# Half of an attention product in rounded parts, the bias as a matrix product, and the experts' data in six loads

## The reference, cut to what matters

```
q, k, v = 1x1 convolutions of x (4 images, 256 channels, 32 x 32 pixels)
energy  = q . k                       # every pixel against every pixel of its image
attn    = softmax(energy, last axis)  # over 32 columns, for each of the 32 rows of keys
x       = gamma * (attn x v) + x
t       = tokens of x                 # 4096 tokens of 256
u       = layer_norm(t)
t       = t + u @ W1 + (memory @ u) @ W2 + bias     # memory: band of 32, within one image
t       = t + mixture of 32 experts, 2 chosen per token, of layer_norm(t)
```

## Time and profile before

| | us |
|---|---|
| median of 3 runs (438.37 to 448.01) | 442.87 |
| the profiled execution's own time | 442.4 |
| its span, first to last instruction | 440.7 |
| PE busy | 371.4 (84%) |
| DVE busy | 331.7 (75%) |
| POOL busy | 286.8 (65%) |
| ACT busy | 272.5 (62%) |

### The profile page before, as it was taken

One profiled execution on the slowest core, in us unless ns is written; L12 is line 12 of the kernel. 1 busy time (PEld: TensorE's weight loads), 2 busy tenths in 40 slices (PEclk: granted clock), 3 DMA queues, 4 the chain that ended last, 5 costly groups with the idle time before them and its releaser, 6 DMA issues. The chain is left out here.

```text
span 440.7 us, 10495 instructions
## 1 busy us (share of the span) xinstructions
PE 371.4 (84%) x2979; PEld 284.1 (64%) x2982; DVE 331.7 (75%) x1032; ACT 272.5 (62%) x817; POOL 286.8 (65%) x377
## 2 busy tenths in 40 slices
PE   8979699999999999999999998867789988767000
PEld 3756478877777877787878787632567777665000
DVE  2865738988888988888999998678578999897010
ACT  1334446776777776677778788670859998845000
POOL 6334425687677787777788888774467777776600
PEclk9999979999999999999999999985999999998555
DMA  6999930114243211123211211122789666531397
GB/s 201 399 199 199 251 85 25 44 56 139 59 171 86 68 56 44 55 78 86 70 59 54 72 56 49 70 75 92 239 250 276 206 204 204 148 110 59 115 233 183
DMA packets 33258, 56.45 MB, mean 128 GB/s; under 512 B 7628, under 2 KB 25502, under 8 KB 32701
## 3 DMA queue, kind: packets, MB, share of 16 engines
q1 hardware_dynamic: 23504, 31.60, 26.4%
q0 software_dynamic: 7488, 21.40, 15.1%
q10 hardware_dynamic: 2208, 2.78, 2.0%
HBM read 33.64 MB, written 24.68 MB: 132 GB/s over the span
## 5 line engine op out<-in xcount | busy, mean ns | idle before, releaser
L1487 PE MATMUL bank<-vT,prob 128*128 128x256 f32 x512 | 118.2, 385 | 1.7 <-POOL prob L623 1.7
L1487 PEld LDWEIGHTS bank<-vT,prob 128*128 128x128 f32 x512 | 96.5, 193 | 14.8 <-POOL prob L623 2.4
L697 POOL DMA_INDIRECT out<-vT,dest x72 | 70.8, 983 | 27.0 <-issue 16.1
L623 POOL TENSOR_TENSOR prob<-prob,ginv 128x1024 f32<-128x1024 f32 x32 | 61.2, 1913 | 23.6 <-DVE ginv L1072 23.6
L600 POOL DMA_INDIRECT slot_rows<-rows,slot x64 | 65.1, 1017 | 17.0 <-issue 15.3
L594 POOL TENSOR_TENSOR rstd<-rstd,half_neg 128x1 f32<-128x1 f32 x64 | 35.7, 558 | 46.1 <-ACT rstd L747 45.8
L808 ACT ACTIVATE prob<-prob 128x1024 f32<-128x1024 f32 x32 | 33.8, 1056 | 20.4 <-DVE prob L1040 20.4
L1036 DVE TENSOR_REDUCE gmax<-X 128x32 f32<-128x1024 f32 x32 | 39.2, 1224 | 7.9 <-PE X L1407 7.8
L1066 DVE TENSOR_REDUCE gsum<-prob 128x32 f32<-128x1024 f32 x32 | 38.7, 1209 | 5.2 <-ACT prob L808 5.1
L1040 DVE TENSOR_TENSOR prob<-X,gmax 128x1024 f32<-128x1024 f32 x32 | 39.2, 1224 | 1.1
L1297 DVE SCALAR_TENSOR_TENSOR vT<-bank,wgt,vT 128x256 f32<-128x256 f32 x72 | 29.9, 477 | 8.8 <-PE bank L1638 6.4
(11 more groups left out here) (235 smaller groups left out, 849.4 us busy)
## 6 DMA issues: line engine op xcount, KB each, us to landing
xt<-x_tok SPq DMA_DIRECT2D x32, 128.0 KB, 2.2
values_s<-values SPq DMA_DIRECT2D x2, 2048.0 KB, 32.6
out<-out POOLq DMA_DIRECT2D x4, 832.0 KB, 15.0
xc_or_xin<-x_cm SPq DMA_DIRECT2D x3, 1024.0 KB, 9.2
t<-x_key SPq DMA_DIRECT2D x3, 1024.0 KB, 9.9
xc_or_xin<-slot_rows SPq DMA_DIRECT2D x20, 130.0 KB
t<-slot_rows SPq DMA_DIRECT2D x16, 130.0 KB
keys_s<-keys SPq DMA_DIRECT2D x1, 2048.0 KB, 18.3
```

Source lines behind the costliest of these rows:

```text
L623: g.tensor_tensor(prob[:, t % 2], prob[:, t % 2], ginv[:, t % 2].unsqueeze(2).to_broadcast([P, WT * KB, W]), ALU.mult).then_inc(prob_done, 1)
L697: g.indirect_dma_start(out=out, out_offset=bass.IndirectOffsetOnAxis(ap=dest[:, n % (2 * NB), k:k + 1], axis=0), in_=yb[:, n % NB, k, :], ...
L1487: mm = m.matmul(av_p, pr[:, j, :], vT[:, b % 2, j, :], start=(j == 0), stop=(j == KB - 1))
```

## The change

Six things change.

1. From tile 8 on, four of the eight blocks of attend are no longer float32 products but three rounded products each. ACT rounds the probabilities of the four blocks (prob_high, 128 x 512, once a tile, ahead of first_squares) and the four blocks of v of an image (value_high, 128 x 256, in four steps of each of three images, behind the exponential). POOL makes the low parts: value_low (128 x 256, behind the scatters) and p_lo (128 x 512, last in its step).
2. POOL's scaling is cut in two halves for these tiles, so that ACT can begin behind the first. PE does the four float32 blocks first and then waits for p_lo.
3. add_bias goes from POOL, last_bias from DVE and the tile t1b with them. The bias is split into a high and a low row and rides in two spare rows of the operand z_end; where a tile has no z_end product, one product with bias_rows is added (7 tiles).
4. Once, in step 2, ACT makes four rows of bias and DVE three.
5. The three loads of 2 MB become six of 1 MB, issued in SP's turns 9, 11, 13, 17, 19 and 21 behind that turn's z_end copies.
6. t2 becomes a ring of four tiles instead of 32, t1 one of four instead of three, with the waits that go with it.

```diff
+EXPERT_LOADS = (9, 11, 13, 17, 19, 21)
...
             for t in range(NT):
-                if t == 4:
-                    sp.dma_start(keys_s[:, :, :, :], keys.rearrange("(a p) e h -> p a e h", p=P)).then_inc(ld_keys, 16)
-                    for side in range(2):
-                        sp.dma_start(values_s[side * HID:(side + 1) * HID, :, :], values).then_inc(ld_keys, 16)
                 if t >= 4:
                     sp.wait_ge(t1_done, t - 3)
                 sp.dma_start(xt[:, t % 4, :], x_tok[t * P:(t + 1) * P, :]).then_inc(ld_xt[t % 4], 16)
                 if end_copied(t - END_COPY):
                     copy_end(t - END_COPY)
+                if t in EXPERT_LOADS:
+                    load_experts(EXPERT_LOADS.index(t))
...
-            def add_bias(t):
...
-                g.tensor_tensor(t1b[:, t % 3], t1[:, t % 3], biasb[:, :], ALU.add).then_inc(t1b_done, 1)
...
             def scale_by_sums(t):
                 pool.wait_ge(inv_done, t + 1)
-                g.tensor_tensor(prob[:, t % 2], prob[:, t % 2],
-                                ginv[:, t % 2].unsqueeze(2).to_broadcast([P, WT * KB, W]), ALU.mult).then_inc(prob_done, 1)
+                if not in_parts(t):
+                    scale_blocks(t, 0, KB, prob_done)
+                else:
+                    scale_blocks(t, 0, SPLIT, half_scaled)
+                    scale_blocks(t, SPLIT, KB, prob_done)
+                    pool.wait_ge(half_scaled, parts_made(t))
+                    pool.wait_ge(p_hi_done, parts_made(t))
+                    after(pool, av_mm, t)
+                    g.tensor_tensor(p_lo[:, :], prob_as(t), p_hi[:, :].bitcast(F32), ALU.subtract).then_inc(p_lo_done, 1)
+
+            def value_low(b, j):
+                pool.wait_ge(v_hi_done, v_parts(b, j))
+                g.tensor_tensor(v_lo[:, b % 2, j, :], vT[:, b % 2, j, :], v_hi[:, b % 2, j, :].bitcast(F32),
+                                ALU.subtract).then_inc(v_lo_done, 1)
...
                 for t in tiles(s, S_TURN):
                     first_factors(t)
-                for t in tiles(s, S_MIX):
-                    add_bias(t)
                 for t in tiles(s, S_SEND + 1):
                     send(t)
+                work = proj_work(s - 1)
+                if work and work[1] < SPLIT:
+                    value_low(work[0], work[1])
                 for t in tiles(s, S_NORM2):
                     second_factors(t)
                 scale_by_sums(s)
...
+            def prob_high(t):
+                act.wait_ge(half_scaled, parts_made(t))
+                after(act, av_mm, t)
+                a.activation(p_hi[:, :], prob_as(t), ACT.Copy).then_inc(p_hi_done, 1)
+
+            def value_high(b, j):
+                act.wait_ge(v_out, v_no(b, j) + 1)
+                a.activation(v_hi[:, b % 2, j, :], vT[:, b % 2, j, :], ACT.Copy).then_inc(v_hi_done, 1)
...
                 a.activation(prob[:, s % 2], prob[:, s % 2], ACT.Exp).then_inc(exp_done, 1)
+                work = proj_work(s - 1)
+                if work and work[1] < SPLIT:
+                    value_high(work[0], work[1])
...
                 for t in tiles(s, S_NORM2):
                     second_factors_kept(t)
+                if in_parts(s):
+                    prob_high(s)
                 for t in tiles(s, S_AV):
                     first_squares(t)
...
                 if end_copied(t - 1):
...
                     terms.append((band_end[:, :], z_end[:, (t - 1) % 2, :]))
-                elif t % TB > 0:
-                    terms += [(band_r[:, P:2 * P], z[:, (t - 1) % 3, :]) for z in (z_hi, z_lo)]
+                else:
+                    pe.wait_ge(bias_done, 3)
+                    terms.append((band_end[:, :], bias_rows[:, :]))
+                    if t % TB > 0:
+                        terms += [(band_r[:, P:2 * P], z[:, (t - 1) % 3, :]) for z in (z_hi, z_lo)]
...
-                for j in range(KB):
-                    mm = m.matmul(av_p, pr[:, j, :], vT[:, b % 2, j, :], start=(j == 0), stop=(j == KB - 1))
+                in_float = range(SPLIT, KB) if in_parts(t) else range(KB)
+                for j in in_float:
+                    mm = m.matmul(av_p, pr[:, j, :], vT[:, b % 2, j, :], start=(j == in_float[0]),
+                                  stop=(j == KB - 1 and not in_parts(t)))
+                if in_parts(t):
+                    pe.wait_ge(v_lo_done, v_parts(b, SPLIT - 1))
+                    pe.wait_ge(p_lo_done, parts_made(t))
+                    for j in range(SPLIT):
+                        at = slice(j * P, (j + 1) * P)
+                        for p_, v_ in ((p_hi, v_hi), (p_hi, v_lo), (p_lo, v_hi)):
+                            mm = m.matmul(av_p, p_[:, at], v_[:, b % 2, j, :], start=False, stop=(j == SPLIT - 1 and p_ is p_lo))
```

More of the change, by code:

```diff
@@ L144, in attention_moe @@
         band_end = sb("band_end", [P, P], F32R)
[L145 to L148, removed]
+        with nc.sbuf_tensor("p_hi", [P, SPLIT * P], F32R) as p_hi, nc.sbuf_tensor("p_lo", [P, SPLIT * P], F32R) as p_lo, \
+                nc.sbuf_tensor("v_hi", [P, 2, SPLIT, C], F32R) as v_hi, nc.sbuf_tensor("v_lo", [P, 2, SPLIT, C], F32R) as v_lo:
+            pass
+        t2_room = sb("t2_room", [P, NT, C])
+        t2 = t2_room[:, NT - 4:]
+        w12 = t2[:, :].rearrange("p (s a) n -> p s a n", s=2)
+        xk = t2_room[:, NT - 4 - TB:NT - 4].rearrange("p (a k) n -> p a (k n)", a=CH)
+        w12_as = t2[:, :].rearrange("p (s a) n -> p a s n", s=2)
         mv2 = sb("mv2", [P, 2, 2])
@@ L362, in quarter_values @@
         def quarter_values(n, k, two):
[L364 removed]
+            return t2_room[:, QV + two * GROUP + k, :] if n == QUARTER_GROUPS else vv_half[:, two, k, :]
         def proj_work(s):
@@ L377, in ends_copied, with in_parts, parts_made, v_parts @@
             return len([n for n in range(t % 2, t + 1, 2) if end_copied(n)])
+        def in_parts(t):
+            return t >= TB
+        def parts_made(t):
+            return t + 1 - TB
+        def v_parts(b, j):
+            return (b - 1) * SPLIT + j + 1
+        def prob_as(t):
+            return prob[:, t % 2, 0:SPLIT * WT].rearrange("p j v -> p (j v)")
         def k_made(b):
@@ L436, in _ @@
             sp.dma_start(gam[:, :], gamma.to_broadcast([P, 1])).then_inc(ld_bcast, 16)
-            sp.dma_start(biasb[:, :], bias.to_broadcast([P, C])).then_inc(ld_bcast, 16)
+            for at in BIAS_AT:
+                sp.dma_start(bias_s[at:at + 1, :], bias).then_inc(ld_bias, 16)
             sp.dma_start(xc[:, 1, :, :], x_cm[:, HW:2 * HW].rearrange(half, p=P)).then_inc(ld_xc[1], 16)
@@ L735, in first_norm @@
                 after(act, uT_mm, t - 1)
-                a.activation(u1[:, t % 2], t1[:, t % 3], ACT.Identity, bias=rstd1[:, t % 2, 2:3],
+                a.activation(u1[:, t % 2], t1[:, t % 4], ACT.Identity, bias=rstd1[:, t % 2, 2:3],
                              scale=rstd1[:, t % 2, 1:2]).then_inc(u1_done, 1)
@@ L777, in second_copy @@
             def second_copy(t):
-                a.activation(rows[:, t % RB, 1, 0:C], t2[:, t], ACT.Identity, bias=rstd2[:, t % 2, 2:3],
+                a.activation(rows[:, t % RB, 1, 0:C], t2[:, t % 4], ACT.Identity, bias=rstd2[:, t % 2, 2:3],
                              scale=rstd2[:, t % 2, 1:2]).then_inc(u2_copied, 1)
@@ L784, in second_norm @@
                 after(act, scattered[t % RB], 32 * (t // RB))
-                a.activation(rows[:, t % RB, 0, 0:C], t2[:, t], ACT.Identity, bias=rstd2[:, t % 2, 2:3],
+                a.activation(rows[:, t % RB, 0, 0:C], t2[:, t % 4], ACT.Identity, bias=rstd2[:, t % 2, 2:3],
                              scale=rstd2[:, t % 2, 1:2]).then_inc(u2_done, 1)
@@ L796, in columns_written, with bias_high @@
                 a.activation(rows[:, t % RB, :, WEIGHT], top[:, t % 4, 0:2], ACT.Copy).then_inc(cols_done, 1)
+            def bias_high():
+                act.wait_ge(end_clear, 3)
+                act.wait_ge(ld_bias, 32)
+                high, low = (slice(at, at + 1) for at in BIAS_AT)
+                for rows_of_bias, source in ((bias_rows[low, :], bias_s[low, :]), (bias_rows[high, :], bias_s[high, :]),
+                                             (z_end[high, 0, :], bias_s[high, :]), (z_end[high, 1, :], bias_s[high, :])):
+                    a.activation(rows_of_bias, source, ACT.Copy).then_inc(bias_hi_done, 1)
+            def prob_high(t):
[5 more added lines that the diff above has]
+                a.activation(v_hi[:, b % 2, j, :], vT[:, b % 2, j, :], ACT.Copy).then_inc(v_hi_done, 1)
             for s in range(NT):
@@ L972, in _ @@
             v.memset(z_end[2 * REACH:P, :, :].bitcast(F32), 0.0)
+            v.memset(bias_rows[:, :].bitcast(F32), 0.0)
             v.memset(band_end[2 * REACH:P, :].bitcast(F32), 0.0).then_inc(end_clear, 1)
+            dve.wait_ge(end_clear, 1)
+            for at in BIAS_AT:
+                v.memset(band_end[at:at + 1, :].bitcast(F32), 1.0).then_inc(end_clear, 1)
             dve.wait_ge(ld_bqk, 16)
```

(7 more changed lines are left out.)

66 lines of the change are left out of this document (35 added, 31 removed).

## The result

The changed kernel takes 449.97 us in the median of 4 runs (446.93 to 451.37), against 444.56 us for 4 runs of the kernel before; the ratio is 1.0211, with a 95% interval of 1.0156 to 1.0266. The two medians as they stand would give 1.012. So the changed kernel is slower; whether by 2% is not decided. The forecast was 449. The profiled execution takes 449.36 us with a span of 447.6. The busy times read: PE 367.7 us (371.4 before), DVE 333.5 (331.7), POOL 308.2 (286.8), ACT 285.8 (272.5).

What follows compares the result with a forecast made beforehand. PE was taken to set the tile loop's pace, with the chain through POOL and ACT about equal in the last image and passing it after the change. 442.4 - 6.6 + 12.0 + 1.0 = 448.8, so 449 us; range 437 to 456.

Steps and rivals of the forecast that it cites:

- The early wait: PE's wait for a z_end copy behind the experts' 6 MB goes with later loads: -6.6 us, bounds 0 to -6.6.
- The chain: POOL and ACT, scaling to scaling: 8.36 us, 8.76 with value_high; 12.0 us more over 23 steps from tile 8 to 31.
- The two bounds on the chain: Scaling halves plus p_lo on POOL at 2.87 or 3.85 us: the 23 steps take 2.4 or 24.9 us more.
- The prices of POOL's operations: POOL's new work priced from profile rows: p_lo 1.27 us, a half scaling 1.05, value_low 0.73.
- Rival 3: The low part is dear: the same chain with 3.85 us on POOL, 461 us in total; chance 0.10.
- PE waiting for the subtraction inside attend: Sign of being right: PE, after attend's float32 blocks of 1.73 us, waits for POOL's p_lo.
- The drain: After tile 31's scaling, POOL reaches the last scatters and factors 1.4 us later: +1.0 us, bounds 0 to +1.5.
- Rival 1: PE goes on setting the tile loop's pace, attend 0.33 us shorter in 24 tiles: 428 us; chance 0.13.
- Rival 2: The z_end wait comes back in SP's queue behind each 1 MB piece: 455 us; chance 0.10.
- Rival 4: Rounded products in attend no faster than float32; hidden by the chain, total unchanged; counted inside the forecast's 0.67.
- the saving in attend: On PE, four float32 blocks become rounded products, 1.73 to 1.40 us: 0.33 us a tile, worth nothing behind the chain.
- PE's steps of 7.7 us: PE's step with shorter attend, about 7.7 us before the last image and 6.9 in it.

Runs made afterwards that it cites:

- e7: The kernel before, unchanged, profiled once more: 438.13 us in one run, tile 8 scaled at 84.87 us.
- e1: The kernel before with only the experts' data in the six later loads: 439.89 us, ratio 0.9911 to the kernel before.
- e4: The changed kernel with p_lo made once, for tile 8, and reused stale by later tiles: 437.7 us, ratio 0.9912 to the kernel before.
- e10: The changed kernel with the subtraction that makes p_lo done twice in each step: 483.87 us in one run.
- e5: The changed kernel with ACT's second_copy moved behind logits_exp: 446.92 us, ratio 1.0142 to the kernel before.
- e2: The changed kernel with the three old 2 MB loads in SP's fifth turn again: 452.4 us, ratio 1.0283 to the kernel before.
- e8: The changed kernel with p_lo behind the first factors and prob_high behind first_squares: 443.79 us, ratio 1.0123 to the kernel before.
- e3: The changed kernel with all attention products in float32, keeping the six loads, PE's bias and the rings: 440.95 us, ratio 1.0025 to the kernel before.
- e9: e5 with rounded parts only in tiles 8 to 23, p_lo and prob_high later, value_low on DVE: 439.24 us, ratio 0.9929 to the kernel before.

## Why the prediction was right

The mechanism held: the chain through POOL and ACT became the bound. That the total came out within 1 us of the forecast is luck in part. In the profiled executions the loop cost 2.4 us and the drain 0.5 us less than forecast, and the experts' stage, costed at nothing, 3.4 us more.

**The early wait, -6.6.** Right for the profiled execution (-6.63), by the mechanism named. As a statement on the kernel it was probably too large: the wait hangs on a few microseconds in the landing of 6 MB, e7 shows 3.3 us, and e1's runs give 3.9 (1.5 to 6.5). One profile can't show how long a wait is in others; the bounds, 0 to -6.6, held.

**The chain, +12.0.** Measured +9.68. That GpSimd and ScalarE become the bound, with ACT waiting for the factors, is shown by e4 and e10 from both sides and by e5, where a piece of ACT alone is moved. The step of the last image came out at 8.35 us where 8.36 was worked out, with two small errors that cancel: the first factors take 1.04 us where 0.93 was put, because their second instruction (L627) went from 0.26 us to 0.40, and scaling, p_lo, ACT and the hand-overs are 0.12 shorter. The 2.4 us too much are in the main in two places. Eight light steps of the middle images took 8.21 us, since that instruction is still 0.26 us there and only the shorter terms are left; that is 8 x 0.15 = 1.2. And the eight value steps took 69.1 us in sum, not 8 x 8.76 = 70.1. There the forecast put value_high on the chain through ACT; what sets the length of those without a projection is POOL's own list, with value_low in it, which the prediction had called covered (e5 leaves it at 8.53). The two bounds on the chain, 2.87 and 3.85 us on POOL, do not take off the 0.08 us by which neighbours overlap, as the 3.29 does; that is 1.8 us in 23 steps, and neither bound was reached.

So the cost lies almost wholly in the last image, 58.33 us for seven steps against 50.45, +7.9; the eight light steps add 1.6, and the eight value steps only 0.2, since half of them hold a projection, where PE's 9.17 us fell to 8.5 to 8.9.

**The prices of POOL's operations.** p_lo 1.275 us where 1.27 was worked out, a half scaling 1.048 where 1.05 was the earlier trace rows. The Trainium skill, GPSIMD Engine Reference, "Elementwise — side-by-side cycle accounting", gave the prediction an estimate of 1.12 for p_lo; the trace, 1.275, does not agree, and the rows decide. Rival 3 falls.

**PE waiting for the subtraction inside attend.** Wrong in its place: the rounded products begin at 245.15, p_lo ended at 244.68. PE waits 1.41 us ahead of memory instead, because z_high comes behind second_norm on ACT. The delay of a closed chain shows on another engine wherever that engine first needs something of it.

**The drain, +1.0.** +0.49, within its bounds. In the other kernels it lies between 37.2 and 39.7 with no order that goes with the change, so a term of this size can't be confirmed.

**The rivals.** Rival 1 (PE keeps the pace) falls: PE is 43.16 of 51 us busy in the last image. Rival 2 falls: no z_end wait comes back. Rival 4 falls: rounded products follow each other every 0.12 us, and the saving in attend (0.22 us where 0.33 was put, since the first of them takes 0.31) is hidden, as forecast. PE's steps of 7.7 us, on which Rival 1 and its 428 us rest, were not reached either: where PE is full they are 7.88 (e4).

**What stays open.** What comes after the drain was costed at nothing and is 3.4 us longer in the profile of after, with more of it at the lower clock, as the rows above show. The experts' stage up to PE's last product took between 95.6 and 104.9 us in the nine profiles of before, after and e2 to e8, with old and new loads and with and without parts, and the granted clock goes with it: 0.98 over 95.6 us in e7, 1.00 over 98.3 in e8, 0.94 over 100.8 in e2, 0.92 over 104.9 in e5. PE's idle time lies between 13.3 and 17.7 us without order. Why the clock is low for longer in some executions, and whether the change has a part in it, was not settled. e1 and e3 reach tile 31 at 265.04 and 265.77, yet their ratios differ by 0.011; one profile of each can't show where that lies. With e1's 3.9 us for the early wait, the sum -3.9 + 9.7 + 0.5 gives +6.3 us, and the ratio, 1.0211, about 9 (6.9 to 11.8): the rest is about the size of the later part in the profile.

## What to carry to other kernels

Before giving an engine more work because its busy share is low, add up the closed chain through it from one start of an operation to its next, and its own list as well: here POOL was busy for 43.38 of 51 us of the last image and waited for another engine only 0.28 us in the step shown. The longest of chain, own list and the full engine sets a step, and taking one below the next buys only the difference (e4's last image: 0.74 us for 1.27; e9: nothing). A wait behind a large transfer that is decided by a few microseconds should be priced from more than one execution, and so should any stage in which the granted clock leaves its upper level.

## What the runs showed of the hardware

The 2 MB loads of values landed 32.6, 30.0 and 29.1 us after issue (medians of two) in the executions of before, e7 and e2, and the wait behind them was 4.05 us, 2.13 us and none. PE stood for 2.13 us in e7 up to 53.53, and behind that the granted clock was at the lower level, 1.2 GHz, as it was behind the 4.05 us of before. Busy time by stretch, e7:

```profile
54.00:56.00 2.00, 2.00 (x8) 1.73 (x8) 0.83 (x4) 1.21 (x3) 0.00 (x0) 0.50 0.40 121
58.00:60.00 2.00, 2.00 (x13) 1.80 (x12) 0.34 (x1) 0.14 (x2) 0.80 (x2) 1.00 0.24 57
```

The second instruction of the first factors on POOL (L627, 128 x 1, the same in each step) took 0.39 to 0.41 us in six steps of the last image of the changed kernel and 0.26 to 0.27 in the third image, and 0.26 to 0.27 in the last image too in e4, e8 and e10; nothing run here says why.
